# Threshold updates per tile, with new orders on ScalarE, GpSimd and TensorE, in a fused linear, top-k and layernorm kernel

## The chip, the cores and the metric

The kernel runs on one core of a Trainium2 chip. The metric is the device time of one execution in microseconds (us), the median of a few runs. The engines are TensorE (PE in the rows, PEld for its weight loads), VectorE (DVE), ScalarE (ACT), GpSimd (POOL) and the DMA queue that SyncE feeds (SP).

## The reference

What is computed, for 4096 tokens of 512 numbers:

```python
x = layernorm(x + x @ (W + delta_W).T)                      # x1
z = x @ ternary(W_syn).T + b_syn                            # 4096 x 2048
thresh = 204th largest of each row of z
hidden = where(z >= thresh, relu(z), 0)
out = hidden @ ternary(W_out).T + b_out
x = layernorm(layernorm(x + out, gamma, beta) + x)
```

`ternary` rounds a matrix to -1, 0 or +1 times its mean absolute value. The first term is one product, since the identity is added to `W + delta_W` in setup.

## The kernel before, in words

The tokens are cut into 32 tiles of 128. After a setup of about 50 us, each engine runs a list of steps written out by hand, a loop over stages `s` from 0 to 36, and works in each stage on several tiles at once: matmul 1 (`mm1`, fp32, 4 matmuls) on tile s+3, matmul 2 (`mm2`, 32 matmuls in two halves c=0 and c=1) on tile s+1, the copy of `z` out of PSUM (`evac`, two halves) on tile s, the selection (`below`, `top8`, `select`, `general`, `hidden`) on tile s-2, and matmul 3 (`mm3_hi` and `mm3_lo`, 16 matmuls each) on tile s-3. Each engine runs its own list strictly in order, and semaphores tie the lists together.

The 204th largest value of a row is searched for. ScalarE counts how many values of a row exceed a threshold (`count`, rounds 0 to 4, one pass over 2048 columns each), the threshold is moved after each count (after round 0 by `first_step` on ScalarE, after 1 to 3 by GpSimd), and VectorE then takes the eight largest values below the last threshold (`below`, `top8`) and picks the right one (`select`). `select` writes `ok`, and PE multiplies it by ones (`flags`), so that VectorE learns in `general` whether every row of the tile was found. Only then comes `hidden`, which zeroes what lies below the threshold. ScalarE rounds the result to fp16 (`hi_h`), VectorE makes the remainder (`lo_h`), and two DMA transposes bring both to `hT` for matmul 3 (their two arrivals are `hiT` and `loT`).

Before the change GpSimd moves the thresholds in a state of three columns, one for each tile in flight: `update_mid` moves one column after round 2, and `update_both` moves all three after the newest tile's round 1 and, with it, the older tile's round 3. A tile's `count` rounds are thereby spread over three stages: 0 and 1 in stage t, 2 and 3 in t+1, 4 in t+2.

Of the kernel before, what the change touches and what calls it, by code (L numbers as in the profile page):

```python
# [39 lines left out]
T_MIN = 1e-18  # L40
# [20 lines left out]
def postln_kernel(nc, x, xT, wT, dwT, w_synT, b_syn, w_outT, b_out, gamma, beta, out):  # L61
    ctx = ExitStack()
    with ctx:
# [155 lines left out]
        def mean_no(s):  # L219
            return s - L_LN2 + 1  # L220

        def count_no(t, r):

            s = t + (0, 0, 1, 1, 2)[r]
            whole = 2 * upto(s - 1) + 2 * upto(s - 2) + upto(s - 3)
            new, old, oldest = live(s), live(s - 1), live(s - 2)
            order = [2] * old + [4] * oldest + [3] * old + [0, 1] * new
            return whole + order.index(r) + 1
# [4 lines left out]
        def _(sp):  # L233
# [50 lines left out]
            for s in range(FIRST, LAST + 1):  # L284
                if live(s - L_MM3):
                    transpose_lo(s - L_MM3)
                if s % 2 and 2 <= (s + 5) // 2 < PAIRS:
                    load((s + 5) // 2)
                if live(s + A_LN1):
                    transpose_x(s + A_LN1)  # L290
                if live(s - L_OUT):
                    store(s - L_OUT)
                if live(s - L_SEL):
                    transpose_hi(s - L_SEL)
# [4 lines left out]
        def _(pool):  # L299
            g = nc.gpsimd  # L300
            made = 0
            for ap, value in ((ident, 0.0), (ones[:, :], 1.0), (cst[:, 0:3], -0.5), (cst[:, 3:4], 0.5),
                              (sums[:, :, :], 0.0), (ss[:, :, :], 0.0), (nmean[:, :, :], 0.0), (t_col[:, :, :], 0.0),
                              (ng[:, :], 0.0), (dev[:, :, :], 0.0), (signs[:, :], 0.0)):
                g.memset(ap, value).then_inc(pool_setup, 1)
                made += 1
# [27 lines left out]
            def means(s):  # L334
                j, d, e = s % 2, s - L_LN2, s - L_OUT
                wait(pool, r_made, upto(d))
                wait(pool, v_made, upto(e))
                wait(pool, sq_done[1], upto(d - 2))
                wait(pool, sq_done[2], upto(e - 2))
                g.tensor_scalar(nmean[:, j, :], sums[:, j, :], -1.0 / D, None, ALU.mult).then_inc(neg_means, 1)  # L340

            def scales(s):
                j, a, d, e = s % 2, s + A_LN1, s - L_LN2, s - L_OUT
                wait(pool, sq_done[0], upto(a))
                wait(pool, sq_done[1], upto(d))
                wait(pool, sq_done[2], upto(e))
# [3 lines left out]
                if live(e):  # L350
                    pool.wait_ge(rs_ready, ln_no(s))
                    g.tensor_tensor(b3[:, j:j + 1], nmean[:, j, 1:2], rs[:, j, 2:3], ALU.mult).then_inc(b3_ready, 1)
# [17 lines left out]
            def update(to, t_old, slope, signed, old, new):  # L370


                q = [tmp[:, k, 0:slope.shape[-1]] for k in range(8)]
                made_dev = step(g.tensor_scalar(new, signed, SIGN_MID, None, ALU.add))  # L374
                pool.wait_ge(update_step, made_dev)
                crossed = step(g.tensor_tensor(q[0], new, old, ALU.mult))
                squared = step(g.tensor_tensor(q[1], new, new, ALU.mult))
                pool.wait_ge(update_step, crossed)
                damp = step(g.tensor_scalar(q[2], q[0], 0.0, -DAMP, ALU.is_lt, ALU.mult))
                pool.wait_ge(update_step, squared)  # L380
                far = step(g.tensor_scalar(q[3], q[1], GATE ** 2, None, ALU.is_gt))
                pool.wait_ge(update_step, damp)
                less = step(g.tensor_tensor(q[4], q[2], slope, ALU.mult))
                pool.wait_ge(update_step, far)
                moved = step(g.tensor_tensor(q[5], q[3], new, ALU.mult))
                pool.wait_ge(update_step, less)
                damped = step(g.tensor_tensor(slope, slope, q[4], ALU.add))
                pool.wait_ge(update_step, max(damped, moved))
                by = step(g.tensor_tensor(q[6], q[5], slope, ALU.mult))  # L389
                pool.wait_ge(update_step, by)  # L390
                at = step(g.tensor_tensor(q[7], t_old, q[6], ALU.add))  # L391
                pool.wait_ge(update_step, at)
                return g.tensor_scalar(to, q[7], T_MIN, None, ALU.max)  # L393

            def update_mid(s, t):

                c = slice(t % CS, t % CS + 1)
                pool.wait_ge(counted, count_no(t, 2))
                update(t_col[:, s % 2, c], t_col[:, s % 2, c], ng[:, c], signs[:, c], dev[:, 1, c], dev[:, 0, c])\
                    .then_inc(updated_mid, 1)  # L400

            def reset(t):

                c = slice(t % CS, t % CS + 1)
                pool.wait_ge(counted, count_no(t, 0))
                step(g.tensor_copy(ng[:, c], start[:, 2:3]))  # L406
                g.tensor_scalar(dev[:, 0, c], sign_first[:, t % 2:t % 2 + 1], SIGN_MID, None, ALU.add).then_inc(t_reset, 1)
                pool.wait_ge(t_reset, t + 1)

            def update_both(s):  # L410

                if live(s):
                    pool.wait_ge(counted, count_no(s, 1))
                else:
                    pool.wait_ge(counted, count_no(s - 1, 3))
                wait(pool, updated_mid, upto(s - 1))
                wait(pool, selected, upto(s - 3))
                update(t_col[:, (s + 1) % 2, :], t_col[:, s % 2, :], ng[:, :], signs[:, :], dev[:, 0, :], dev[:, 1, :])\
                    .then_inc(updated, 1)

            for s in range(FIRST, LAST + 1):
                if s <= 2 and live(s + A_LN1):
                    scales(s)
                if s == -A_LN1:
                    bias_norm()
                if s == 0:
                    sigma()
                    scale_vecs()
# [5 lines left out]
                if live(s - L_SEL):  # L434
                    pool.wait_ge(masked, s - L_SEL + 1)
                if live(l):
                    if l == 0:
                        pool.wait_ge(vecs_made, 1)
                    add_bout(l)
                if live(d):  # L440
                    add_beta(d)
                if live(s):
                    reset(s)
                if live(s) or live(s - 1):
                    update_both(s)
                if live(d) or live(d - 1):
                    means(s + 1)

        @block.scalar
        def _(act):  # L450
# [51 lines left out]
            def count(s, t, r):  # L502
                if r == 0:
# [459 lines left out]
```

## Time and profile before

| | |
|---|---|
| median of 3 runs | 734.36 us (734.27 to 737.39) |
| the profiled execution | 738.88 us, span 736.8 us |
| busy: PE, DVE, ACT, POOL | 594.3, 542.7, 543.5, 470.4 us |
| mean granted TensorE clock | 0.943 of full |
| length of a stage in the steady part | 19.63 us |

The profiled execution lies 4.5 us above the median of the runs. Busy times overlap, so that they don't add up to the span; what bounds the kernel has to be read from the waits inside one stage. A row of the timeline gives the start, the duration, the engine, the line, the operation with what it writes and reads, and in brackets how long the engine had been idle and what ended that.

### The profile page before, as it was taken

How to read it: one execution, taken by the hardware profiler on the slowest of the kernel's cores; microseconds unless marked ns; L12 is line 12 of the kernel's file. 1: busy time of each engine (PE TensorE's matmuls, PEld its weight loads, DVE VectorE, ACT ScalarE, POOL GpSimd, SP SyncE). 2: the span in 40 equal slices, each digit the busy share in tenths (PEclk: the TensorE clock that was granted, in tenths of full speed). 3: DMA queues.
4: the chain of work that ended last, by engine and by line, in shares of the span. 5: the costliest groups of instructions: out<-in, count | busy, mean ns of one | idle time of the engine just before them, and what ended most of it. 6: DMA issues, size and time to landing. Idle time of an engine off the chain costs nothing.

```text
span 736.8 us, 8563 instructions
## 1 busy us (share of the span) xinstructions
PE 594.3 (81%) x2374; PEld 254.3 (35%) x2374; DVE 542.7 (74%) x650; ACT 543.5 (74%) x695; POOL 470.4 (64%) x1016
## 2 busy tenths in 40 slices
PE   0586579998888898899989899988888889874443
PEld 0132224443333333333333334433333333331111
DVE  4568486977777778788877777777777788886651
ACT  2753766778888888888888888888888888777422
POOL 0128556776767777776676677666676776676521
PEclk9988789999999999999999999999999999986676
DMA  8922034344455445555454443436454445433331
GB/s 347 384 53 59 0 64 95 65 99 72 108 86 115 79 97 82 115 87 115 86 111 90 81 101 73 98 79 116 85 94 86 80 86 86 86 72 72 71 74 40
DMA packets 184482, 71.63 MB, mean 97 GB/s; under 512 B 168048, under 2 KB 176240, under 8 KB 183792
## 3 DMA queue, kind: packets, MB, share of 16 engines
q1 hardware_dynamic: 184432, 71.07, 44.6%
q8 instruction: 19, 0.31, 0.2%
q14 instruction: 31, 0.25, 0.1%
HBM read 20.72 MB, written 8.39 MB: 40 GB/s over the span
## 4 chain that ended last, share of the span: by engine, by line
issue 33%; ACT 27%; POOL 24%; PE 7%; DMA 6%; DVE 2%; ACTq 1%; SPq 0%; POOLq 0%; DVEq 0%
ACT junk L525 12%; POOL tmp L389 8%; PE o_ps L886 3%; ACT y_sb L547 3%; POOL t_col L393 3%; DMA hT<-hh 2%; ACT junk_ln L499 2%; ACT x1s L537 2%; DMA z_sb<-in_w_synT 2%; ACT junk_ln L491 2%; POOL dev L374 2%; ACT junk_ln L483 2%; PE o_ps L892 2%; POOL tmp L391 2%; ACT t_col L531 2%
## 5 line engine op out<-in xcount | busy, mean ns | idle before, releaser
L525 ACT ACTIVATE junk<-z_sb,t_col 128x2048 f16<-128x2048 f32 x128 | 255.7, 1998 | 115.6 <-POOL t_col L393 114.5
L876 PE MATMUL z_ps<-t_syn,xhT 128*128 128x512 f16 x1024 | 231.1, 384 | 8.9 <-DMA xhT<-xh 6.4
L886 PE MATMUL o_ps<-t_out,hT 128*128 128x512 f16 x512 | 127.3, 406 | 76.3 <-DMA hT<-hh 76.3
L862 PE MATMUL u_ps<-weff,xT_sb 128*128 128x512 f32 x256 | 126.2, 638 | 34.3 <-ACT x1s L537 17.4
L876 PEld LDWEIGHTS z_ps<-t_syn,xhT 128*128 128x128 f16 x1024 | 101.2, 99 | 143.3 <-issue 33.3
L892 PE MATMUL o_ps<-t_out,hT 128*128 128x512 f16 x512 | 115.7, 379 | 0.5 <-DMA hT<-hh 0.5
L374 POOL TENSOR_SCALAR dev<-signs 128x3 f32<-128x3 f32 x65 | 63.5, 977 | 79.0 <-ACT junk L525 58.3
L886 PEld LDWEIGHTS o_ps<-t_out,hT 128*128 128x128 f16 x512 | 50.4, 103 | 151.8 <-DMA hT<-hh 84.6
L779 DVE SCALAR_TENSOR_TENSOR z_sb<-z_sb,thr 128x2048 f32<-128x2048 f32 x32 | 75.5, 2360 | 29.2 <-DVE flag L758 20.7
L406 POOL COPY ng<-start 128x1 f32<-128x1 f32 x32 | 50.9, 1591 | 65.4 <-ACT junk L525 65.4
L745 DVE SCALAR_TENSOR_TENSOR z_sb<-z_ps,sc,bias_z 128x1024 f32<-128x1024 f32 x64 | 79.5, 1277 | 14.8 <-PE z_ps L876 14.6
L752 DVE TENSOR_TENSOR xh<-x1s,xh 128x512 f16<-128x512 f32 x32 | 34.9, 1092 | 69.4 <-ACT xh L542 69.4
L713 DVE TENSOR_TENSOR hh<-z_sb,hh 128x2048 f16<-128x2048 f32 x32 | 73.3, 2292 | 12.4 <-ACT hh L554 12.0
L554 ACT ACTIVATE hh<-z_sb 128x2048 f16<-128x2048 f32 x32 | 60.7, 1897 | 26.8 <-DVE z_sb L779 26.7
L862 PEld LDWEIGHTS u_ps<-weff,xT_sb 128*128 128x128 f32 x256 | 49.2, 203 | 88.1 <-issue 87.9
L719 DVE SCALAR_TENSOR_TENSOR w_sb<-z_sb,t_col 128x2048 f32<-128x2048 f32 x32 | 75.0, 2345 | 0.3
L724 DVE MAX8 m<-w_sb 128x8 f32<-128x2048 f32 x32 | 73.4, 2295 | 1.1
L389 POOL TENSOR_TENSOR tmp<-tmp,ng 128x3 f32<-128x3 f32 x65 | 67.9, 1045 | 5.1
L892 PEld LDWEIGHTS o_ps<-t_out,hT 128*128 128x128 f16 x512 | 50.0, 98 | 61.2 <-DMA hT<-hh 1.0
L525 ACT ACTIVATE junk<-z_sb,start 128x2048 f16<-128x2048 f32 x32 | 63.7, 1989 | 1.0 <-DVE z_sb L745 1.0
L347 POOL TENSOR_SCALAR var<-ss 128x3 f32<-128x3 f32 x39 | 8.1, 207 | 53.8 <-ACT junk_ln L483 44.4
L357 POOL TENSOR_TENSOR x1b<-x1s,vecs 128x512 f32<-128x512 f32 x32 | 40.6, 1268 | 0.3 <-issue 0.2
(117 smaller groups left out, 640.1 us busy)
## 6 DMA issues: line engine op xcount, KB each, us to landing
xT_sb<-in_xT SPq DMA_DIRECT2D x16, 512.0 KB, 4.6
out_y<-y_sb SPq DMA_DIRECT2D x32, 256.0 KB, 2.4
z_sb<-in_w_synT SPq DMA_DIRECT2D x4, 1024.0 KB, 13.6
hh<-in_w_outT SPq DMA_DIRECT2D x2, 1024.0 KB, 18.9
z_sb<-in_w_outT SPq DMA_DIRECT2D x2, 1024.0 KB, 13.7
weff<-in_wT SPq DMA_DIRECT2D x1, 1024.0 KB, 5.7
w_sb<-in_dwT SPq DMA_DIRECT2D x1, 1024.0 KB, 7.9
bias_z<-in_b_syn SPq DMA_DIRECT2D x1, 1024.0 KB, 17.7
```

The costliest lines, as they stand in the source:

```text
L374: made_dev = step(g.tensor_scalar(new, signed, SIGN_MID, None, ALU.add))
L389: by = step(g.tensor_tensor(q[6], q[5], slope, ALU.mult))
L525: a_.activation(junk[:, n % 2, :], z_sb[:, t % ZS, :], ACT.Sign, bias=at, scale=-1.0, accum_out=signed)\
L713: v.tensor_tensor(hh[:, j, 1, :], z_sb[:, t % ZS, :], hh[:, j, 0, :], ALU.subtract).then_inc(h_lo, 1)
L719: v.scalar_tensor_tensor(w_sb[:, :], z, t_col[:, t % 2, t % CS:t % CS + 1], z, ALU.is_le, ALU.mult)\
L724: v.max(out=m8[:, t % 2, :], in_=w_sb[:, :]).then_inc(max8_done, 1)
L745: v.scalar_tensor_tensor(z_sb[:, t % ZS, c * HALF:(c + 1) * HALF], z_ps[:, c, :], sc[:, 7:8], bias_z[:, c * HALF:(c + 1) * HALF], ALU.mult ...
L779: v.scalar_tensor_tensor(z, z, thr[:, t % 2:t % 2 + 1], z, ALU.is_ge, ALU.mult).then_inc(h_made, 1)
L862: last = mm(u_ps[:, :], xT_sb[:, j, k, (t % 2) * P:(t % 2 + 1) * P], weff[:, k, :], start=k == 0, stop=k == KD - 1)
L876: last = mm(z_ps[:, c, b * BANK:(b + 1) * BANK], xhT[:, j, h * KD + k, :], t_syn[:, k, n0:n0 + BANK], start=k == 0 and h == 0, stop=k == K ...
L886: mm(o_ps[t % OS][:, :], hT[:, j, 0, c, :], t_out[:, c, :], start=c == 0, stop=False)
L892: last = mm(o_ps[t % OS][:, :], hT[:, j, 1, c, :], t_out[:, c, :], start=False, stop=c == KN - 1)
```

## The change

Each tile gets threshold state of its own (`t_col`, `slope`, `dev` and `signs` with a column for each round). `update(t, r)` replaces `update_mid` and `update_both`: seven instructions on one column for each of rounds 1, 2 and 3, where there were eleven, two times a stage. `reset` shrinks to `first_dev`. Round 4 now follows in stage t+1.

```diff
+            def update(t, r):
+                ...
+                pool.wait_ge(counted, count_no(t, r))
+                ...
+                crossed = step(g.tensor_scalar(q[0], signed, SIGN_MID, old, ALU.add, ALU.mult))
                 made_dev = step(g.tensor_scalar(new, signed, SIGN_MID, None, ALU.add))
+                pool.wait_ge(update_step, crossed)
+                damp = step(g.tensor_scalar(q[1], q[0], 0.0, -DAMP, ALU.is_lt, ALU.mult))
+                ...
+                g.tensor_scalar(t_col[:, j, r + 1:r + 2], q[3], slope[:, j, r:r + 1], t_col[:, j, r:r + 1],
+                                ALU.mult, ALU.add).then_inc(updated[r - 1], 1)
```

GpSimd's stage, before and after (`means` and `scales` now serve the second layernorm one stage earlier, tile s-3 in place of s-4, and the third tile s-4 in place of s-5; the wait for `masked` ahead of `add_bout` is gone; `scale_vecs` moves to VectorE in setup):

```diff
-                if live(s - 1):
-                    update_mid(s, s - 1)
-                if s > 2 and (live(s + A_LN1) or live(s - L_LN2) or live(s - L_OUT)):
-                    scales(s)
-                l, d = s + 1 - L_MM3, s + 1 - L_LN2
-                if live(s - L_SEL):
-                    pool.wait_ge(masked, s - L_SEL + 1)
...
-                    add_bout(l)
...
-                    add_beta(d)
...
-                    reset(s)
...
-                    update_both(s)
...
-                    means(s + 1)
+                if live(s - 1):
+                    update(s - 1, 3)
+                if live(l) or live(d):
+                    means(s)
+                if live(l):
+                    add_beta(l)
                 if live(s):
+                    first_dev(s)
+                    update(s, 1)
+                if live(l + 1):
...
+                    add_bout(l + 1)
+                if live(s + A_LN1) or live(l) or live(d):
                     scales(s)
                 if live(s):
+                    update(s, 2)
```

TensorE's stage:

```diff
                     mm3_hi(l)
-                    mm3_lo(l)
                 if live(f):
                     flags(s, f)
+                if live(l):
+                    mm3_lo(l)
                 if live(s + A_MM1):
                     mm1(s + A_MM1)
```

On VectorE the order of a stage stays (`lo_h`, both `evac`, `below`, `top8`, `select`, `lo_x`, `general`, `hidden`, then the layernorm steps); in the first stages one `sum_out` leaves it for ScalarE and `scale_vecs` comes. SyncE issues the transpose of `hi_h` ahead of the store and no longer behind it.

TensorE in the steady part, before the change. `u_ps` is matmul 1, `z_ps<-t_syn` matmul 2, `o_ps` matmul 3 (the two kinds of line are its high and its low half), `z_ps<-ok` the flags:

```order
66 L886 MATMUL o_ps<-t_out,hT 128x512 [waits y_ready,hiT1]
67 L886 MATMUL o_ps<-t_out,hT 128x512 x15
68 L892 MATMUL o_ps<-t_out,hT 128x512 [waits loT1]
69 L892 MATMUL o_ps<-t_out,hT 128x512 x15
70 L900 MATMUL z_ps<-ok,ones 1x1 [waits flag_read,z_evac,selected]
71 L862 MATMUL u_ps<-weff,xT_sb 128x512 [waits x1_ready,x_loaded0]
72 L862 MATMUL u_ps<-weff,xT_sb 128x512 x3
73 L876 MATMUL z_ps<-t_syn,xhT 128x512 [waits z_evac,flag_read,xT_done1]
```

The same engine with the change:

```order
44 L851 MATMUL o_ps<-t_out,hT 128x512 [waits hiT1]
45 L851 MATMUL o_ps<-t_out,hT 128x512 x15
46 L865 MATMUL z_ps<-ok,ones 1x1 [waits flag_read,z_evac,selected]
47 L857 MATMUL o_ps<-t_out,hT 128x512 [waits loT1]
48 L857 MATMUL o_ps<-t_out,hT 128x512 x15
49 L827 MATMUL u_ps<-weff,xT_sb 128x512 [waits x1_ready,x_loaded1]
50 L827 MATMUL u_ps<-weff,xT_sb 128x512 x3
51 L841 MATMUL z_ps<-t_syn,xhT 128x512 [waits z_evac,flag_read,xT_done1]
```

The flags matmul, with its wait for `selected`, now stands between the two halves of matmul 3; it stood behind both.

ScalarE in one steady stage before (`junk` rows are counts, `hh` is `hi_h`, `junk_ln` the squares, `x1s` and `xh` the first layernorm and its fp16 half, `y_sb` the output):

```order
101 L525 ACTIVATE junk,signs<-z_sb,t_col 128x2048
102 L525 ACTIVATE junk,sign_last<-z_sb,t_col 128x2048
103 L483 ACTIVATE junk_ln,ss<-u_ps 128x512
104 L491 ACTIVATE junk_ln,ss<-o_ps1,nmean 128x512
105 L499 ACTIVATE junk_ln,ss<-o_ps0,nmean 128x512
106 L525 ACTIVATE junk,signs<-z_sb,t_col 128x2048
107 L537 ACTIVATE x1s<-u_ps,rs 128x512
108 L542 ACTIVATE xh<-x1s 128x512
109 L547 ACTIVATE y_sb<-o_ps0,b3,rs 128x512
110 L525 ACTIVATE junk,sign_first<-z_sb,start 128x2048
111 L531 ACTIVATE t_col<-sign_first,start 128x1
112 L525 ACTIVATE junk,signs<-z_sb,t_col 128x2048
```

And with the change:

```order
100 L493 ACTIVATE junk,signs<-z_sb,start 128x2048
101 L493 ACTIVATE junk,signs<-z_sb,t_col 128x2048
102 L499 ACTIVATE t_col<-signs,start 128x1
103 L522 ACTIVATE hh<-z_sb 128x2048
104 L515 ACTIVATE y_sb<-o_ps0,b3,rs 128x512
105 L493 ACTIVATE junk,signs<-z_sb,t_col 128x2048 x2
106 L471 ACTIVATE junk_ln,ss<-o_ps1,nmean 128x512
107 L463 ACTIVATE junk_ln,ss<-o_ps2,nmean 128x512
108 L455 ACTIVATE junk_ln,ss<-u_ps 128x512
109 L493 ACTIVATE junk,signs<-z_sb,t_col 128x2048
110 L505 ACTIVATE x1s<-u_ps,rs 128x512
111 L510 ACTIVATE xh<-x1s 128x512
```

The newest tile's first count moved to the front, each tile's counts are separated by other work, and `hi_h` stands fourth where it stood last.

## Rows read from the trace of the kernel before

**Rows 1.** Busy time by stage: PE, PEld, DVE, ACT, POOL (instructions), PEclk, DMA share, GB/s
```profile
398.31:417.94 19.63, 17.77 (x76) 7.71 (x74) 15.54 (x18) 16.22 (x21) 13.84 (x31) 1.00 0.47 81
...
614.19:633.82 19.63, 15.95 (x68) 6.64 (x67) 15.53 (x18) 16.22 (x22) 13.84 (x31) 0.91 0.40 80
```

**Rows 2.** Who waited for whom: us in total, times, longest
```profile
ACT junk L525 <- POOL t_col L393: 114.5, 62, 7.7
```

**Rows 3.** Timeline of one steady stage, the wait on ScalarE
```profile
398.32 2.29 DVE L713 TENSOR_TENSOR hh<-z_sb,hh 128x2048 f16<-128x2048 f32 x1 [0.41 <-ACT hh L554]
398.43 2.24 POOL L389 TENSOR_TENSOR tmp<-tmp,ng 128x3 f32<-128x3 f32 x1
...
401.30 2.00 ACT L525 ACTIVATE junk<-z_sb,t_col 128x2048 f16<-128x2048 f32 x1 [3.02 <-POOL t_col L393]
```

**Rows 4.** Timeline, VectorE from the second evac to the selection
```profile
128.97 1.28 DVE L745 SCALAR_TENSOR_TENSOR z_sb<-z_ps,sc,bias_z 128x1024 f32<-128x1024 f32 x1 [1.66 <-PE z_ps L876]
130.18 2.34 DVE L719 SCALAR_TENSOR_TENSOR w_sb<-z_sb,t_col 128x2048 f32<-128x2048 f32 x1
132.55 2.29 DVE L724 MAX8 m<-w_sb 128x8 f32<-128x2048 f32 x1
134.88 0.22 DVE L731 TENSOR_SCALAR_CACHE_REDUCE pick<-place,sign_last 128x8 f32<-128x8 f32 x1
135.15 0.23 DVE L734 SCALAR_TENSOR_TENSOR ok<-m,t_col,hit 128x1 f32<-128x1 f32 x1
```

**Rows 5.** Timeline, TensorE in the same stretch
```profile
118.33 3.70 PE L862 MATMUL u_ps<-weff,xT_sb 128*128 128x512 f32 x8
121.87 7.07 PE L876 MATMUL z_ps<-t_syn,xhT 128*128 128x512 f16 x32
128.77 3.62 PE L886 MATMUL o_ps<-t_out,hT 128*128 128x512 f16 x16
132.23 3.62 PE L892 MATMUL o_ps<-t_out,hT 128*128 128x512 f16 x16
135.77 0.19 PE L900 MATMUL z_ps<-ok,ones 128*1 128x1 f32 x2
135.89 3.70 PE L862 MATMUL u_ps<-weff,xT_sb 128*128 128x512 f32 x8
```

**Rows 6.** Timeline, stage 2: selection, flags, and the wait before them
```profile
91.29 0.22 DVE L734 SCALAR_TENSOR_TENSOR ok<-m,t_col,hit 128x1 f32<-128x1 f32 x1
...
91.56 0.19 PE L900 MATMUL z_ps<-ok,ones 128*1 128x1 f32 x2 [8.61 <-DVE ok L734]
```

**Rows 7.** Timeline, TensorE at the end: idle gaps and what followed
```profile
610.21 7.07 PE L876 MATMUL z_ps<-t_syn,xhT 128*128 128x512 f16 x32
618.75 3.63 PE L886 MATMUL o_ps<-t_out,hT 128*128 128x512 f16 x16 [1.47 <-DMA hT<-hh]
...
628.16 8.75 PE L876 MATMUL z_ps<-t_syn,xhT 128*128 128x512 f16 x32 [2.21 <-issue]
...
645.86 7.07 PE L876 MATMUL z_ps<-t_syn,xhT 128*128 128x512 f16 x32 [0.29 <-issue]
656.79 6.40 PE L886 MATMUL o_ps<-t_out,hT 128*128 128x512 f16 x16 [3.87 <-DMA hT<-hh]
...
715.53 6.05 PE L886 MATMUL o_ps<-t_out,hT 128*128 128x512 f16 x16 [9.88 <-DMA hT<-hh]
```

**Rows 8.** Timeline, TensorE in the first stages
```profile
60.97 0.38 PE L904 MATMUL o_ps<-part_out,ones 128*128 128x1 f32 x2 [1.59 <-DVE part_out L694]
...
69.44 6.61 PE L862 MATMUL u_ps<-weff,xT_sb 128*128 128x512 f32 x8 [4.62 <-ACT x1s L537]
```

**Rows 9.** DMA issues: median us from issue to landing
```profile
hT<-hh SPq DMA_TRANSPOSE x3, 4.4
```

**Rows 10.** Timeline, the last full stages: general, hidden and hi_h
```profile
628.92 2.35 DVE L779 SCALAR_TENSOR_TENSOR z_sb<-z_sb,thr 128x2048 f32<-128x2048 f32 x1 [0.86 <-DVE flag L758]
...
631.95 1.90 ACT L554 ACTIVATE hh<-z_sb 128x2048 f16<-128x2048 f32 x1
```

More of the change, by code:

```diff
@@ L219, in mean_no @@
         def mean_no(s):
-            return s - L_LN2 + 1
+            return s - L_MM3 + 1
         def count_no(t, r):
[L224 to L227, printed above, removed]
+            s = t + (r > 2)
+            whole = 3 * upto(s - 1) + 2 * upto(s - 2)
+            new, old = [0] * live(s), [3] * live(s - 1)
+            order = new + old + [1] * live(s) + [4] * live(s - 1) + [2] * live(s)
             return whole + order.index(r) + 1
@@ L368, in step, with first_dev @@
                 return steps_made[0]
-            def update(to, t_old, slope, signed, old, new):
-                q = [tmp[:, k, 0:slope.shape[-1]] for k in range(8)]
+            def first_dev(t):
+                pool.wait_ge(counted, count_no(t, 0))
+                g.tensor_scalar(dev[:, t % 2, 0:1], signs[:, t % 2, 0:1], SIGN_MID, None, ALU.add).then_inc(dev_made, 1)
+            def update(t, r):
+                j = t % 2
+                signed, new, old = signs[:, j, r:r + 1], dev[:, j, r:r + 1], dev[:, j, r - 1:r]
+                before = slope[:, j, r - 1:r] if r > 1 else start[:, 2:3]
+                q = [tmp[:, k:k + 1] for k in range(4)]
+                pool.wait_ge(counted, count_no(t, r))
+                if r == 1:
+                    pool.wait_ge(dev_made, t + 1)
+                crossed = step(g.tensor_scalar(q[0], signed, SIGN_MID, old, ALU.add, ALU.mult))
@@ L380, in update @@
+                pool.wait_ge(update_step, damp)
+                damped = step(g.tensor_scalar(slope[:, j, r:r + 1], q[1], before, before, ALU.mult, ALU.add))
                 pool.wait_ge(update_step, squared)
[L381 to L408, printed above, removed]
@@ new lines, in update @@
+                far = step(g.tensor_scalar(q[3], q[2], GATE ** 2, new, ALU.is_gt, ALU.mult))
+                pool.wait_ge(update_step, max(damped, far))
+                if r == ROUNDS - 2:
+                    wait(pool, selected, t - 1)
+                g.tensor_scalar(t_col[:, j, r + 1:r + 2], q[3], slope[:, j, r:r + 1], t_col[:, j, r:r + 1],
+                                ALU.mult, ALU.add).then_inc(updated[r - 1], 1)
+                pool.wait_ge(updated[r - 1], t + 1)
+            scales(-3)
@@ L601, in _ @@
                 if live(s):
-                    count(s, s, 0)
-                    first_step(s, s)
-                    count(s, s, 1)
-                if live(f):
-                    hi_h(f)
+                    count(s, 1)
+                if live(s - 1):
+                    count(s - 1, 4)
+                if live(d):
+                    square3(s, d)
+                if live(l):
+                    square2(s, l)
+                if live(a):
+                    square1(s, a)
+                if live(s):
+                    count(s, 2)
+                if live(a):
+                    ln1_out(s, a)
+                    hi_x(a)
         @block.vector
@@ L819, in _ @@
                     evac(s, 0)
+                    evac(s, 1)
                 if s == 1:
@@ L822, in _ @@
                     out_weights(0)
-                if live(s):
-                    evac(s, 1)
-                if s == 0:
-                    lo_x(a)
-                    sum_out(2)
-                    sum_out(3)
-                    out_part()
-                if s == 1:
-                    lo_x(a)
-                    out_weights(1)
                 if live(f):
@@ L836, in _ @@
                     select(f)
-                if live(a) and s > 1:
+                if live(a):
                     lo_x(a)
-                if s == 2:
-                    out_weights(2)
+                if s == 0:
+                    sum_out(3)
+                    scale_vecs()
+                    out_part()
+                if s == 1:
+                    out_weights(1)
                 if live(f):
```

228 lines of the change are left out of this document (98 added, 130 removed).

## The prediction, made before the changed kernel ran

> **What bounds the kernel now.** I read the busy times by stage first. In a steady stage PE is busy 17.77 us of 19.63, ScalarE 16.22, VectorE 15.54, GpSimd 13.84 [rows 1]: no engine is full, so a loop of waits sets the pace. The list of waits puts 114.5 us on ScalarE, in 62 waits for a threshold from GpSimd [rows 2]. The timeline shows one: ScalarE idles 3.02 us until `update_both` is through [rows 3]. One small GpSimd instruction of that chain takes 2.24 us, while VectorE's `lo_h` of 2.29 us runs beside it [rows 3]. So today's loop runs through ScalarE's counts and GpSimd's two updates, and PE, 1.47 us idle per stage before matmul 3, is close behind [rows 7]. The GPSIMD Engine Reference of the Trainium skill, section 1 (Specifications), says that GpSimd shares its SBUF interfaces with VectorE, with contention where VectorE has two SBUF inputs; the stretched row agrees.
>
> The steady pace to compare with: matmul 2 of one tile ends at 121.87 + 7.07 = 128.94 and that of the tile 25 stages later at 610.21 + 7.07 = 617.28 [rows 5, 7], so 19.53 us a stage.
>
> **The change, part by part.** *GpSimd and ScalarE.* The two updates of eleven instructions become three of seven, on one column, and ScalarE has other work between the counts of one tile. I cost the ScalarE stall as gone: the engine's own work of 16.22 us [rows 1] is then its floor, and GpSimd's 13.84 falls by what is no longer stretched. This cover holds as long as a stage lasts longer than about 16.5 us. The early place of `hi_h` makes ScalarE wait for `hidden` of the same stage. Behind it are queued `ln3_out`, two counts, the squares, the last count, `x1s` and `xh`; VectorE's next `lo_h` and matmul 3 wait for it. From `lo_h` to the end of `hidden` VectorE has lo_h 2.29, two evacs 2.47 (1.21 pitch and 1.28), below and max8 4.70, select about 0.7, lo_x 0.7 to 1.1, the flag 1.0 and hidden 2.35, some 14.4 us; with `hi_h`, 1.90 [rows 3, 4, 10], that loop needs about 16.4 us. It doesn't bind while another loop needs more.
>
> *TensorE.* This part decides. `flags` waits for `select` of tile s-2, which VectorE makes after the second `evac` of the stage, `below` and `top8`. And that evac waits for the end of matmul 2, the last thing PE did in its stage before. Before the change PE had both halves of matmul 3 to do in the meantime: they begin at 128.77 and PE reaches the flags at 135.77, while `select` is ready at 135.15 + 0.23 = 135.38 [rows 4, 5]. The wait cost nothing, by 0.4 us. Now only the high half stands ahead of it, and PE must stand idle; `mm3_lo`, `mm1` and `mm2` are queued behind, and VectorE's next second evac waits for those. This closes a loop of exactly one stage:
> - second evac to `ok`: from 128.97 to 135.15, and 0.23: 6.41 us [rows 4]
> - `ok` to the flags: 91.56 - 91.29 - 0.22 = 0.05 [rows 6]
> - flags to the next matmul: 0.12 [rows 5]
> - `mm3_lo`: 3.46, the pitch of 16 such matmuls from 128.77 to 132.23 [rows 5]
> - `mm1`: 3.54, from 118.33 to 121.87 [rows 5]
> - `mm2`: 7.07, and 0.03 until the evac [rows 4, 5]
>
> Together 20.68 us, against 19.53 now: +1.15 in each of 25 steady stages, +28.8 us. Without the move of the flags this loop would be 20.68 - 3.46 = 17.2 us. Nothing on GpSimd and ScalarE can shorten it, and both have over 4 us of room in it.
>
> *The clock of TensorE.* In this loop PE stands idle in every stage from 128.77 + 3.62 = 132.39 (end of the high half) until the flags at 128.97 + 6.41 + 0.05 = 135.43: 3.04 us. The trace shows the granted clock 1.00 with gaps of 1.47 us, 25 times [rows 1, 7]. After a gap of 2.21 us the next 32 matmuls took 8.75 us instead of 7.07 (+1.68), in the stage with a granted clock of 0.91 [rows 1, 7]; after 3.87 us the next 16 took 6.40 instead of 3.63 (+2.77) [rows 7]. These are stretches of the 1.2 GHz level in place of 2.4. The new gap lies between the two that were followed by a fall. The bounds are 0 and 2.77 per stage; I take 1.68. The new gap is as far from the one row as from the other (0.83 us each), and I choose the cheaper, because it leaves room for stages in which the clock doesn't fall: 25 x 1.68 = +42.0 us. TensorE: Matmul & The Clock Gate of the Trainium skill, section "HAM oscillation", warns of a kernel that went back to the slower clock in each pass of its loop, since it waited in each; this is the rule that speaks against the change, and the rows above agree with it.
>
> *Stages 29 and 30* have no `mm1` left: 20.68 - 3.54 + 1.68 = 18.82 each, together 37.6. Before it is from 617.28 to 645.86 + 7.07 = 652.93, or 35.65 [rows 7]: +2.0 us.
>
> *The first stages.* PE waited 4.62 us for `x1s`, which stood behind a count that waited for GpSimd, and 1.59 us for `part_out`, behind a `sum_out` that now goes to ScalarE [rows 8]. Before the first flags it waited 8.61 [rows 6]; the path from matmul 2 to `ok` needs 6.49 as above, so 2.1 comes off. Together -8.3 us. The bounds are 0 (new waits in their place) and -14.8, all three waits gone whole; I take the sum since GpSimd now has fewer and shorter steps there.
>
> *The end.* After the last matmul 2 (652.93) nothing fills PE. The four high halves of matmul 3 follow until 715.53 [rows 7], 62.6 us. Each tile's counts now end a stage earlier, so that ScalarE and GpSimd no longer hold the chain. After the last matmul 2: 6.5 to the flags, about 1.2 to `hidden`, 2.35, `hi_h` 1.90, the transpose 4.4, so 16.4 to the high half of tile 29. For tiles 30 and 31 each: high half 6.2 (of 6.40 and 6.05), flags and general 1.3, hidden 2.35, hi_h 1.95, transpose 4.4, so 16.2 [rows 4, 7, 9, 10]. In sum 48.8: -13.8 us. Behind tile 31's matmul 3 I leave the chain as it is (736.8 - 715.53 = 21.3). Bounds: 0 and -18.
>
> SyncE's transpose ahead of the store, and `means` and `scales` one stage earlier, I cost at nothing: the transpose arrives 4.4 us after its issue [rows 9], and PE wants it over 8 us later in a stage of 20.7. `add_bout`, which no longer waits for `masked`, falls into VectorE's idle time before the second evac; if it met `below` it could hold it 1.3 us, on the loop.
>
> **Sum.** +28.8 +42.0 +2.0 -8.3 -13.8 = +50.7 us. The profiled execution, 738.88 us, would become 789.6; against the median of the runs, 734.36, it gives **785 us**.
>
> **The rivals.**
> - *The clock stays up.* Same loop, no fall: 785 - 42 - 3 = 740, up to about 750 with a fall now and then. For it: the gap moves in time from stage to stage, and 1.47 us never did harm. Against it: both gaps over 2 us. Some 20%, and 10% for something between, 750 to 773.
> - *The clock falls longer*, 2.77 a stage: 785 + 27 x 1.1 = 815. 4%.
> - *PE doesn't wait at the flags (the other sign).* If `select` were ready when the high half ends, that is within 3.5 us of the end of matmul 2, in place of 6.5, the ScalarE stall would be all that changed, and PE's own 17.77 with some 0.4 us of seams would set the pace: 18.2 a stage, 734 - 25 x 1.35 - 22 = 678. For it: the stall of 3.02 us really goes. Against it: evac 1.21, below 2.37 and max8 2.33 stand in VectorE's list ahead of `select` [rows 4], unchanged. It decides if that order, or the wait of the second evac for matmul 2, were not as I read them. 5%.
> - *GpSimd's chain still binds*, since VectorE's long instructions stretch its small ones: that would need over 4 us more a stage than now. 2%; it would add to the 785.
>
> **How the numbers follow.** The forecast with the fall in nearly every stage has 60%, with 774 to 797 as its own range (first stages and end off by a few us each, the clock's price 1.3 to 2.0). About 0.5% is what a measurement of this kernel tells from no change, 730.7 to 738.0 us. Faster: 6% (the PE rival and an end better than I think). Same: 5% (clock up, first stages or end better by 5 us). Slower: 89%. The range reaches down to the case of the steady clock, 741, and up to 799; about 2 in 10 lie outside.
>
> **What would show it.** In the changed kernel's profile: PE idle about 3 us ahead of the flags in each stage, ended by VectorE's `ok`; ScalarE's long wait for `t_col` gone, replaced by a wait for `hidden` at `hi_h`; VectorE idle some 2 us ahead of the second evac, ended by matmul 2; a granted clock below 1.00 in the steady stages, and `mm3_lo` or `mm1` sometimes long. A stage of 22.4 us shows the whole, 20.7 the loop alone. Wrong would be a pace under 20 us, or the wait ahead of the flags ended by something else than `ok`.

## The result, and the profile after

The changed kernel takes **778.67 us** (median of four runs, 765.82 to 781.07), against 734.32 for the kernel before on the same chip: a ratio of 1.049 (95% interval 1.036 to 1.062). The ratio is made from the two quicker runs, 776.42 and 765.82 us, whose median is 771.12, so that the 65 and 23 us worked out below from the median of all four would be 58 and 16 against these. TensorE's mean granted clock was 0.909, 0.909, 0.913 and 0.929 in the four runs, in the order of falling time. The forecast was 785 us, with a range of 741 to 799, and a chance of 89% for slower. The profiled run took 780.93 us, with a span of 779.1.

The page of the changed kernel: busy time, the granted clock in 40 slices, and the chain that ended last.
```profile
PE 614.4 (79%) x2374; PEld 262.6 (34%) x2374; DVE 527.0 (68%) x649; ACT 546.6 (70%) x697; POOL 539.9 (69%) x936
...
PEclk9789789999999999999999999999999999997666
...
PE 55%; DVE 22%; POOL 8%; issue 8%; DMA 3%; ACT 2%; DVEq 0%; POOLq 0%; SPq 0%; ACTq 0%
PE z_ps L841 24%; PE o_ps L857 16%; PE u_ps L827 13%; DVE w_sb L687 8%; DVE m L692 8%; PE o_ps L851 2%; POOL t_col L392 1%; POOL dev L380 1%; DMA hT<-hh 1%; DMA xhT<-xh 1%; DMA w_sb<-in_dwT 1%; POOL tmp L379 1%; DVE pick L700 1%; ACT junk L493 1%; DVE ok L703 1%
```
The chain names the loop by itself, all but the second `evac`, whose time it counts as issue: `mm2` (L841), `below` (L687), `max8` (L692), `ok` (L703), `mm3_lo` (L857), `mm1` (L827). The high half of matmul 3 (L851) stands in it with 2% only, since it lies beside VectorE's part.

Who waited for whom, the changed kernel: us in total, times, longest.
```profile
DVE z_sb L714 <- PE z_ps L841: 153.5, 57, 5.5
ACT hh L522 <- DVE z_sb L748: 103.7, 29, 7.8
PE z_ps L865 <- DVE ok L703: 91.0, 30, 6.5
...
ACT junk L493 <- POOL t_col L392: 60.1, 39, 5.3
```
ScalarE's 114.5 us for a threshold [rows 2] have become 60.1, in shorter pieces; its long wait is now for `hidden` at `hi_h` (L522). PE waits 91.0 us, 30 times, for `ok` at the flags.

The timeline of TensorE in the changed kernel, three stages.
```profile
352.17 7.07 PE L841 MATMUL z_ps<-t_syn,xhT 128*128 128x512 f16 x32
359.07 3.62 PE L851 MATMUL o_ps<-t_out,hT 128*128 128x512 f16 x16
365.72 0.19 PE L865 MATMUL z_ps<-ok,ones 128*1 128x1 f32 x2 [3.03 <-DVE ok L703]
365.84 5.31 PE L857 MATMUL o_ps<-t_out,hT 128*128 128x512 f16 x16
370.99 3.60 PE L827 MATMUL u_ps<-weff,xT_sb 128*128 128x512 f32 x8
374.43 7.07 PE L841 MATMUL z_ps<-t_syn,xhT 128*128 128x512 f16 x32
...
387.98 0.19 PE L865 MATMUL z_ps<-ok,ones 128*1 128x1 f32 x2 [3.03 <-DVE ok L703]
388.10 5.07 PE L857 MATMUL o_ps<-t_out,hT 128*128 128x512 f16 x16
...
396.44 7.07 PE L841 MATMUL z_ps<-t_syn,xhT 128*128 128x512 f16 x32
...
410.00 0.19 PE L865 MATMUL z_ps<-ok,ones 128*1 128x1 f32 x2 [3.03 <-DVE ok L703]
410.12 3.63 PE L857 MATMUL o_ps<-t_out,hT 128*128 128x512 f16 x16
```
In each stage PE stands idle 3.03 us ahead of the flags. Then `mm3_lo` takes 3.63 us, or 5.31, or 5.07: after two of three gaps the clock is down for a while. From matmul 2 to matmul 2 the stages last 22.26, 22.01 and, without a fall, 20.57 us, in this order again and again.

By stretch, the changed kernel: 25 steady stages, stages 29 and 30, and the end (columns as in [rows 1]).
```profile
120.49:662.93 542.44, 466.63 (x1851) 201.51 (x1850) 377.40 (x450) 407.63 (x527) 410.93 (x702) 0.94 0.42 83
662.93:698.90 35.97, 29.90 (x132) 12.69 (x130) 29.66 (x35) 25.09 (x29) 27.44 (x44) 0.95 0.30 58
698.90:779.00 80.10, 37.19 (x134) 14.20 (x134) 41.98 (x55) 35.63 (x50) 47.53 (x76) 0.71 0.33 70
```
The sum on the spans of the two profiled runs (736.8 to 779.1 us, +42.3), each part beside what was forecast:

| part | before | after | difference | forecast |
|---|---|---|---|---|
| start, to the end of tile 4's matmul 2 | 128.94 | 120.49 | -8.45 | -8.3 |
| 25 steady stages | 488.34 | 542.44 | +54.1 | +70.8 |
| of it the loop, 25 x (20.57 - 19.53) | | | +26.0 | +28.8 |
| of it the clock, the rest | | | +28.1 | +42.0 |
| stages 29 and 30 | 35.65 | 35.97 | +0.3 | +2.0 |
| the end | 83.9 | 80.2 | -3.7 | -13.8 |

### The profile page after: what moved, and what is told of

It is laid out like the page before. It is cut to its first block, busy times and chain, and to the rows that moved or that the text cites. A ratio compares the mean times of both kernels' runs of the same rounds, so it can differ in the third digit from the quotient of the medians.

```text
span 779.1 us, 8524 instructions
## 1 busy us (share of the span) xinstructions
PE 614.4 (79%) x2374; PEld 262.6 (34%) x2374; DVE 527.0 (68%) x649; ACT 546.6 (70%) x697; POOL 539.9 (69%) x936
## 4 chain that ended last, share of the span: by engine, by line
PE 55%; DVE 22%; POOL 8%; issue 8%; DMA 3%; ACT 2%; DVEq 0%; POOLq 0%; SPq 0%; ACTq 0%
PE z_ps L841 24%; PE o_ps L857 16%; PE u_ps L827 13%; DVE w_sb L687 8%; DVE m L692 8%; PE o_ps L851 2%; POOL t_col L392 1%; POOL dev L380 1%; DMA hT<-hh 1%; DMA xhT<-xh 1%; DMA w_sb<-in_dwT 1%; POOL tmp L379 1%; DVE pick L700 1%; ACT junk L493 1%; DVE ok L703 1%
## 5 line engine op out<-in xcount | busy, mean ns | idle before, releaser
L493 ACT ACTIVATE junk<-z_sb,t_col 128x2048 f16<-128x2048 f32 x128 | 255.4, 1996 | 61.2 <-POOL t_col L392 60.1
L841 PE MATMUL z_ps<-t_syn,xhT 128*128 128x512 f16 x1024 | 228.7, 382 | 5.0 <-DMA xhT<-xh 5.0
L714 DVE SCALAR_TENSOR_TENSOR z_sb<-z_ps,sc,bias_z 128x1024 f32<-128x1024 f32 x64 | 82.0, 1283 | 153.5 <-PE z_ps L841 153.5
L851 PE MATMUL o_ps<-t_out,hT 128*128 128x512 f16 x512 | 126.0, 403 | 34.6 <-DMA hT<-hh 34.6
L841 PEld LDWEIGHTS z_ps<-t_syn,xhT 128*128 128x128 f16 x1024 | 100.5, 98 | 138.3 <-issue 26.2
L857 PE MATMUL o_ps<-t_out,hT 128*128 128x512 f16 x512 | 145.8, 449 | 0.0
L827 PE MATMUL u_ps<-weff,xT_sb 128*128 128x512 f32 x256 | 124.1, 630 | 22.6 <-DVE weff L608 16.8
L522 ACT ACTIVATE hh<-z_sb 128x2048 f16<-128x2048 f32 x32 | 61.1, 1909 | 103.7 <-DVE z_sb L748 103.7
L379 POOL TENSOR_SCALAR tmp<-signs,dev 128x1 f32<-128x1 f32 x96 | 68.9, 718 | 89.2 <-ACT junk L493 80.7
L335 POOL TENSOR_SCALAR nmean<-sums 128x2 f32<-128x2 f32 x33 | 62.2, 1886 | 49.3 <-DVE o_ps L769 47.5
L851 PEld LDWEIGHTS o_ps<-t_out,hT 128*128 128x128 f16 x512 | 52.1, 103 | 104.1 <-DMA hT<-hh 31.6
L857 PEld LDWEIGHTS o_ps<-t_out,hT 128*128 128x128 f16 x512 | 55.0, 112 | 76.5 <-issue 39.2
L865 PE MATMUL z_ps<-ok,ones 128*1 128x1 f32 x64 | 6.0, 164 | 91.0 <-DVE ok L703 91.0
L827 PEld LDWEIGHTS u_ps<-weff,xT_sb 128*128 128x128 f32 x256 | 51.4, 203 | 78.1 <-issue 74.4
L687 DVE SCALAR_TENSOR_TENSOR w_sb<-z_sb,t_col 128x2048 f32<-128x2048 f32 x32 | 76.0, 2376 | 0.5 <-POOL t_col L392 0.5
L692 DVE MAX8 m<-w_sb 128x8 f32<-128x2048 f32 x32 | 73.4, 2295 | 1.1
L388 POOL TENSOR_SCALAR tmp<-tmp,dev 128x1 f32<-128x1 f32 x96 | 63.9, 666 | 9.4
L386 POOL TENSOR_SCALAR slope<-tmp,slope 128x1 f32<-128x1 f32 x64 | 62.4, 974 | 0.0
L392 POOL TENSOR_SCALAR t_col<-tmp,slope,t_col 128x1 f32<-128x1 f32 x96 | 44.4, 462 | 9.5
```

The source lines that it names most:

```text
L379: crossed = step(g.tensor_scalar(q[0], signed, SIGN_MID, old, ALU.add, ALU.mult))
L388: far = step(g.tensor_scalar(q[3], q[2], GATE ** 2, new, ALU.is_gt, ALU.mult))
L493: a_.activation(junk[:, n % 2, :], z_sb[:, t % ZS, :], ACT.Sign, bias=at, scale=-1.0, accum_out=signs[:, j, r:r + 1]).then_inc(counted, 1)
L687: v.scalar_tensor_tensor(w_sb[:, :], z, t_col[:, t % 2, ROUNDS - 1:ROUNDS], z, ALU.is_le, ALU.mult)\
L692: v.max(out=m8[:, t % 2, :], in_=w_sb[:, :]).then_inc(max8_done, 1)
L714: v.scalar_tensor_tensor(z_sb[:, t % ZS, c * HALF:(c + 1) * HALF], z_ps[:, c, :], sc[:, 7:8], bias_z[:, c * HALF:(c + 1) * HALF], ALU.mult ...
```

## The experiments

All change one thing in the changed kernel, if not said otherwise. The kernel before ran beside each of them, with medians of 733.94 (the first four), 735.64 (`e5` to `e8`), 737.19 (`e9`) and 735.24 us (`e10`, `e11`).

**e1_flags_behind: the one suspected part undone.**
```diff
                     mm3_hi(l)
+                    mm3_lo(l)
                 if live(f):
                     flags(s, f)
-                if live(l):
-                    mm3_lo(l)
```


> The changed kernel with the flags matmul put back behind both halves of matmul 3, everything else of the change kept. My theory (the early flags close a loop of 20.6 us): PE's idle time ahead of the flags (91 us in the changed kernel) goes, the loop falls to about 17.1 us, PE's own work sets the pace, about 18.2 us a stage at a granted clock of 1.00, and the time is some 680 to 695 us, below the kernel before. Rival (the new ScalarE and GpSimd orders are what slows the kernel): it stays above 750 us.

Measured: 713.52 us (712.22 to 714.59), ratio 0.972 (0.968 to 0.976). With the flags back in their old place the change makes the kernel *quicker* than before, by 2.8%. The place of the flags is worth 778.67 - 713.52 = 65 us, and all the rest of the change, without it, about -20. Yet it isn't the 680 to 695 that I had expected. The timeline of three engines in one stage:
```profile
395.73 0.26 POOL L379 TENSOR_SCALAR tmp<-signs,dev 128x1 f32<-128x1 f32 x1 [2.37 <-ACT junk L493]
...
397.70 2.46 POOL L392 TENSOR_SCALAR t_col<-tmp,slope,t_col 128x1 f32<-128x1 f32 x1
...
403.05 2.33 POOL L384 TENSOR_SCALAR tmp<-dev 128x1 f32<-128x1 f32 x1
...
406.58 2.00 ACT L493 ACTIVATE junk<-z_sb,t_col 128x2048 f16<-128x2048 f32 x1 [2.37 <-POOL t_col L392]
...
408.27 0.88 POOL L344 TENSOR_TENSOR rs<-var,cst 128x3 f32<-128x3 f32 x1
409.18 0.69 ACT L505 ACTIVATE x1s<-u_ps,rs 128x512 f32<-128x512 f32 x1 [0.51 <-POOL rs L344]
410.01 3.67 PE L827 MATMUL u_ps<-weff,xT_sb 128*128 128x512 f32 x8 [0.85 <-ACT x1s L505]
...
414.32 0.19 ACT L493 ACTIVATION_READ_ACCUMULATOR junk<-z_sb,t_col 128x1 f32 x1
```
PE no longer waits for `ok`, but for `x1s`. A new loop of one stage binds. GpSimd does update 3, `means`, `add_beta`, `first_dev`, update 1, `add_bout` and `scales` with hardly a pause, from 395.73 until `rs` is there at 409.15, 13.4 us; two of its small instructions are stretched to 2.46 and 2.33 us where they elsewhere take 0.34 and 0.29. ScalarE has waited 0.51 us for `rs` and then does `x1s`, `xh` and the next stage's first two counts, from 409.18 to 414.51, 5.3 us; the second of these counts starts GpSimd's next update 3. With the seams that is the stage, 18.95 us in most of them, and no longer PE's 18.2. ScalarE's longer wait, 2.37 us for the threshold, lies inside this loop and does not set its pace: behind it ScalarE still waited for `rs`.

**e2_before_flags_mid: this part done alone, in the kernel before** (the diff of `e1` turned round).

> The kernel before with only the flags matmul moved between the two halves of matmul 3. My theory: the same loop of 20.6 us arises there, PE waits 3 us ahead of the flags in each stage and its clock falls in most; pace 21.5 to 22, time 780 to 800 us. Rival: the old update chain of 19.6 us with its slack hides the move, 734 to 745 us.

Measured: 775.96 us (773.10 to 778.15), ratio 1.056 (1.051 to 1.061), a little under the 780 to 800 that I had expected. Its timeline of TensorE:
```profile
413.97 0.19 PE L900 MATMUL z_ps<-ok,ones 128*1 128x1 f32 x2 [3.03 <-DVE ok L734]
414.10 5.32 PE L892 MATMUL o_ps<-t_out,hT 128*128 128x512 f16 x16
```
The same gap, and the same stages of 20.58, 22.26 and 22.01 us. Once this loop binds, nothing that the rest of the change does to ScalarE and GpSimd is seen in the steady stages.

**e3_fill12 and e8_fill6: the clock apart from the loop.** Ahead of the high half PE does 12 (or 6) of its matmuls once more; the next start overwrites them, so that the output is the same.
```diff
                 wait(pe, y_ready, t - OS + 1)
+                for c in range(12):
+                    mm(o_ps[t % OS][:, :], hT[:, j, 0, c, :], t_out[:, c, :], start=c == 0, stop=c == 12 - 1)
                 for c in range(KN):
```


> The changed kernel with 12 matmuls more ahead of the high half of matmul 3 (a repetition of its first 12, overwritten by the real ones), so that PE works 2.6 of the 3.03 us in which it waited for the flags. The loop isn't touched, only the idle time. If the clock's fall is a cost of its own: granted clock 1.00 in the steady stages, stages of 20.6 us, time 745 to 755 us. Rival (the long low halves come from something else, say the flags matmul or memory traffic): 775 or more.

> The changed kernel with 6 matmuls more ahead of the high half of matmul 3, which leaves 1.75 us of idle time ahead of the flags, between the 1.47 us that left the clock up and the 2.21 us after which it fell once. If a gap must be near 2.2 us: granted clock 1.00 in the steady stages and 750 to 757 us. If the fall begins below that: some low halves of 5 us, 757 to 775.

Measured: 755.55 us with 12 (754.64 to 757.35), ratio 1.028 (1.025 to 1.032), at the upper end of what I had expected, and 754.07 with 6 (one run), as expected. The timeline of TensorE with 12:
```profile
411.09 2.75 PE L851 MATMUL o_ps<-t_out,hT 128*128 128x512 f16 x12
413.68 3.62 PE L853 MATMUL o_ps<-t_out,hT 128*128 128x512 f16 x16
417.74 0.19 PE L867 MATMUL z_ps<-ok,ones 128*1 128x1 f32 x2 [0.44 <-DVE ok L703]
417.86 3.63 PE L859 MATMUL o_ps<-t_out,hT 128*128 128x512 f16 x16
```
and with 6:
```profile
414.88 0.19 PE L867 MATMUL z_ps<-ok,ones 128*1 128x1 f32 x2 [1.74 <-DVE ok L703]
415.00 3.63 PE L859 MATMUL o_ps<-t_out,hT 128*128 128x512 f16 x16
```
More work in the gap and less time: each stage is now 20.57 us, at a granted clock of 1.00. That is the loop without the clock, and the clock's share is 778.67 - 755.55 = 23 us. A gap of 1.74 us leads to no fall either.

**e4_flags_first: a larger dose**, the flags ahead of both halves.
```diff
+                if live(f):
+                    flags(s, f)
                 if live(l):
...
                     mm3_hi(l)
-                if live(f):
-                    flags(s, f)
-                if live(l):
                     mm3_lo(l)
```


> The changed kernel with the flags matmul ahead of both halves of matmul 3: a larger dose. My theory: the loop grows by 3.46 us to 24.0 and PE's idle time ahead of the flags to 6.5 us, a fall of the clock in every stage adds 1.5 to 3; pace 25.5 to 27, time 870 to 910 us. If the loop were not the cause, the time would stay near 780 us.

Measured: 905.71 us (one run), within the 870 to 910 expected, granted clock 0.843. The timeline of TensorE:
```profile
395.97 0.19 PE L865 MATMUL z_ps<-ok,ones 128*1 128x1 f32 x2 [6.48 <-DVE ok L703]
396.09 4.97 PE L851 MATMUL o_ps<-t_out,hT 128*128 128x512 f16 x16
```
The whole path from matmul 2 to `ok` is now a gap, 6.48 us, as the forecast's 6.41 of VectorE and its seams say. Stages last 25.4, 26.3 and 26.8 us, and now the clock falls in each.

**e5_tail: the end.** The end had gained 3.7 us in place of 13.8. The changed kernel's timeline after its last matmul 2 shows where `hi_h` stood:
```profile
707.30 2.36 DVE L748 SCALAR_TENSOR_TENSOR z_sb<-z_sb,thr 128x2048 f32<-128x2048 f32 x1 [1.22 <-issue]
707.61 2.14 POOL L380 TENSOR_SCALAR dev<-signs 128x1 f32<-128x1 f32 x1
...
711.54 2.00 ACT L493 ACTIVATE junk<-z_sb,t_col 128x2048 f16<-128x2048 f32 x1 [3.13 <-POOL t_col L392]
713.82 1.89 ACT L522 ACTIVATE hh<-z_sb 128x2048 f16<-128x2048 f32 x1
720.04 6.34 PE L851 MATMUL o_ps<-t_out,hT 128*128 128x512 f16 x16 [10.58 <-DMA hT<-hh]
```
`hidden` was ready at 709.66, but `hi_h` began 4.2 us later, queued behind round 3 of tile 30's counts, which waited for a GpSimd update that `hidden` itself had stretched (2.14 us for a small instruction). The experiment puts `hi_h` ahead of that count, from stage 31 on.
```diff
                     count(s, 0)
+                if live(f) and s >= TILES - 1:
+                    hi_h(f)
                 if live(s - 1):
                     count(s - 1, 3)
...
-                if live(f):
+                if live(f) and s < TILES - 1:
                     hi_h(f)
```


> The changed kernel with hi_h moved ahead of count round 3 on ScalarE in the last stages alone (from stage 31). My theory of the missing gain at the end: hidden of tiles 29 and 30 was done at 709.7 and 729.9 us, but hi_h began 4.1 and 4.2 us later, behind a count that waited for GpSimd. Then the stretch from the last matmul 2 to the end shrinks from 80.2 to about 72 us. Rival (the transposes or the slow clock of matmul 3 set the end): within 1.5 us of 80.

Measured: 777.12 us (one run), and 75.2 us from the end of the last matmul 2, against 80.2: neither the 72 of my theory nor the rival's 80. The high half of tile 29 comes 16.8 us after matmul 2 (forecast 16.4). But tile 30's waits for `y_sb`, since `ln3_out` is now what stands behind the count that waits for GpSimd:
```profile
733.07 2.00 ACT L493 ACTIVATE junk<-z_sb,t_col 128x2048 f16<-128x2048 f32 x1 [3.79 <-POOL t_col L392]
...
735.97 5.00 PE L853 MATMUL o_ps<-t_out,hT 128*128 128x512 f16 x16 [9.37 <-ACT y_sb L515]
```
So 5 of the missing 10 us are shown to be this queue. Of the rest, tile 30 took 2.8 us more than forecast, with this wait for `y_sb` ahead of it, and tile 31 1.8 us more, which was not followed up.

**e6, e7, e9, e10, e11: GpSimd's order, all on top of e1.** These ask whether the loop of 18.95 us can be cut. `e10` and `e11` ran on another chip than the rest. GpSimd's order in a stage of `e1` is update 3, means, add_beta, update 1, add_bout, scales, update 2.
- `e6_beta_late`: add_beta behind update 1. `e7_beta_tail`: the same, with the edit of `e5`
- `e9_scales_early`: update 1, scales, add_bout, add_beta, update 2
- `e10_bout_between`: update 1, scales, add_bout, update 2, add_beta
- `e11_adds_last`: update 1, scales, update 2, add_bout, add_beta

The edit of `e6`; the others are of the same kind.
```diff
-                if live(l):
-                    add_beta(l)
                 if live(s):
                     first_dev(s)
                     update(s, 1)
+                if live(l):
+                    add_beta(l)
```


> The changed kernel with the flags behind both halves of matmul 3, and on GpSimd add_beta behind update(s, 1) in place of ahead of it. With the flags back a stage took 18.95 us, and ScalarE waited 2.37 us for update(s, 1), which stood behind add_beta (1.27 us) and was then stretched by below (2.33). My theory: that wait sets the pace there; it goes, PE's own 17.8 and seams take over, 18.2 to 18.5 a stage, time 698 to 706 us. Rival (DMA arrival of hT or the hidden, hi_h, lo_h loop sets it): 711 to 715.

> The kernel of the run before with hi_h ahead of count round 3 in the last stages too. If both theories hold: 6 to 9 us below it, 690 to 699. If the end is set by something else: the same time.

> The changed kernel with the flags behind both halves of matmul 3, and on GpSimd both adds (add_bout, then add_beta) behind update(s, 1) and scales(s). With add_beta late alone the wait moved: ScalarE's wait for update(s, 1) fell from 2.37 to 1.20 us, but its wait for rs from scales rose from 0.51 to 1.78, and the pace stayed at 18.9. My theory: GpSimd's order, with its instructions stretched by VectorE, still sets the pace; with scales early too the x1s step comes 1.5 us or more sooner and the pace falls to 18.0 to 18.4, 694 to 703 us. Rival (DMA arrival of hT, or the hidden, hi_h, lo_h loop): 709 to 714 again.

> Flags behind both halves, GpSimd's stage in the order update 3, means, update 1, scales, add_bout, update 2, add_beta. In the run before, update 2 began behind both adds at 413.4 us and fell under hidden (one step of 0.34 took 2.46), so that count round 3, hi_h and lo_h came 3 us late and the pace was 20.7. My theory: with one add behind update 2 it is through before hidden begins, while scales stays early: pace 18.0 to 18.5, 695 to 704 us. If an early scales itself were what hurt: 745 to 755 again. If something off GpSimd holds the pace at 18.9: 710 to 714.

> The same with both adds behind update 2. My theory: update 2 is early, but now update 3 of the next stage stands behind the adds; as it is not urgent (its count has 6 us until select), 695 to 706 us, near the run with add_bout between. If update 3 is what matters: 712 or more.

| kernel | us | range | ratio to before |
|---|---|---|---|
| e6_beta_late | 712.72 | 711.96 to 714.63 | 0.970 (0.965 to 0.974) |
| e7_beta_tail | 712.22 | 711.90 to 717.04 | 0.970 (0.965 to 0.976) |
| e9_scales_early | 753.46 | 752.01 to 754.08 | 1.024 (1.021 to 1.026) |
| e10_bout_between | 722.13 | 720.82 to 724.55 | 0.983 (0.979 to 0.986) |
| e11_adds_last | 719.58 | 719.44 to 719.72 | 0.978 (0.976 to 0.981) |

None of the five met the forecast of my theory; `e6`, `e7` and `e11` came out at the time given for another cause. Two waits on ScalarE's timeline of `e6` show why the first did nothing:
```profile
405.41 2.00 ACT L493 ACTIVATE junk<-z_sb,t_col 128x2048 f16<-128x2048 f32 x1 [1.20 <-POOL t_col L392]
...
409.29 0.69 ACT L505 ACTIVATE x1s<-u_ps,rs 128x512 f32<-128x512 f32 x1 [1.78 <-POOL rs L344]
```
The wait for the threshold fell from 2.37 to 1.20 us, and that for `rs`, whose `scales` stood behind the moved addition, rose from 0.51 to 1.78. The sum stays (2.88 and 2.98), and so does the pace, 19.0 us: the loop goes through `rs` and `x1s`, as it did in `e1`, and ahead of `rs` nothing had been taken away. My number for the rival (711 to 715) was met, by this cause and not the one I had named. At the end `e7` took 84.5 us for the 84.1 of `e6`: no gain.

The timeline of `e9` shows what an order can cost:
```profile
411.30 0.74 DVE L703 SCALAR_TENSOR_TENSOR ok<-m,t_col,hit 128x1 f32<-128x1 f32 x1
411.97 1.31 DVE L705 SCALAR_TENSOR_TENSOR pick<-place,signs,m 128x8 f32<-128x8 f32 x1
...
414.81 2.35 DVE L748 SCALAR_TENSOR_TENSOR z_sb<-z_sb,thr 128x2048 f32<-128x2048 f32 x1 [0.86 <-DVE flag L727]
414.92 2.46 POOL L386 TENSOR_SCALAR slope<-tmp,slope 128x1 f32<-128x1 f32 x1
...
418.26 2.00 ACT L493 ACTIVATE junk<-z_sb,t_col 128x2048 f16<-128x2048 f32 x1 [3.62 <-POOL t_col L392]
...
422.46 2.29 DVE L681 TENSOR_TENSOR hh<-z_sb,hh 128x2048 f16<-128x2048 f32 x1 [3.10 <-ACT hh L522]
...
426.78 3.63 PE L851 MATMUL o_ps<-t_out,hT 128*128 128x512 f16 x16 [3.00 <-DMA hT<-hh]
```
Update 2, now behind both additions, falls beside `hidden`, one of its small instructions takes 2.46 us, and the delay runs through the count, `hi_h` and `lo_h` to PE: 20.74 us in this stage, 18.1 to 23.7 in the steady ones. VectorE is held up as well: beside GpSimd's two additions (`add_bout` from 410.76, `add_beta` from 411.99) `ok` took 0.74 us and the `pick` behind it 1.31, in place of 0.22 each in `e1`. `e10` differs from `e9` only in that update 2 stands ahead of `add_beta`, and gets 31 us back. So the order of these two is shown to be the cause; whether by the late update 2 or by the longer `pick`, which is back at 0.22 us in `e10`, is not told apart. `e10` and `e11` stay above `e1`. In `e10` it is `add_beta` that meets `hidden`:
```profile
417.12 2.39 DVE L748 SCALAR_TENSOR_TENSOR z_sb<-z_sb,thr 128x2048 f32<-128x2048 f32 x1 [1.24 <-issue]
417.46 3.19 POOL L356 TENSOR_TENSOR x1g<-x1s,vecs 128x512 f32<-128x512 f32 x1
```
The quickest kernels of all are `e1`, `e6` and `e7`, whose ranges overlap.

## Why the prediction was right, point by point

- **The loop through the flags.** Right, and shown by undoing it (`e1`, -65 us), doing it alone (`e2`, +42) and the larger dose (`e4`, +127). The gap was 3.03 us (forecast 3.04) and the stage without a fall 20.57 (20.68). The rival in which PE doesn't wait is out.
- **The clock, 1.68 in each stage.** Right in kind and too large in size, the term most off: +28.1 us in the profiled run and 23 by `e3` (its extra matmuls also lengthen the end, 83.6 us for 80.2), not 42.0. A fall costs what I took, 1.69 or 1.44, but comes after two gaps of three. I had put "nearly every stage" on record as the likeliest, with the row of 2.21 us, a single case, as its only price. The section on HAM oscillation in TensorE: Matmul & The Clock Gate of the Trainium skill speaks of a fall in each pass; here it was two in three at 3.03 us, and each at 6.48.
- **The rival "the clock stays up"** (740 to 750) did not come. The run of 765.82 us, at a granted clock of 0.929, falls in the range of the case between (750 to 773, 10%). No profile of it was kept, so how often the clock fell in it is not known.
- **ScalarE's stall "gone".** Partly. 60.1 us of waits for `t_col` are left. They cost nothing in steady stages as long as a stage lasts 20.6 us, for those of `e2` are as long; in `e1` GpSimd's loop binds. Here the forecast's floor was wrong: it held the cover to last down to 16.5 us a stage, from ScalarE's busy time and the loop through `hi_h`. The loop of GpSimd's updates, additions and `rs` with ScalarE's `x1s` and counts needs 18.95, and I had not added it up: the room in a stage of 20.57 was 1.6 us, and not over 4. The case of 678 us shared this fault: without the wait at the flags the kernel takes 713.5.
- **The first stages.** -8.45 for -8.3, in part by luck. The wait ahead of the first flags was 6.49 us, as worked out; that for `part_out` is gone, and that for `x1s` fell from 4.62 to 0.66 us. But `mm1` behind it took 3.67 us in place of 6.61 [rows 8], 2.9 us that I had not counted. A new wait of 1.57 us for `x1s`, a longer `mm1` behind it (6.58 for 5.75) and small losses at the first matmul 3 took about as much away.
```profile
62.60 3.67 PE L827 MATMUL u_ps<-weff,xT_sb 128*128 128x512 f32 x8 [0.66 <-ACT x1s L505]
...
81.42 6.58 PE L827 MATMUL u_ps<-weff,xT_sb 128*128 128x512 f32 x8 [1.57 <-ACT x1s L505]
```
- **The end.** -3.7 for -13.8: the step "ScalarE and GpSimd no longer hold the chain" failed. `hi_h` stood behind a count that waited for GpSimd, which accounts for 5 of the missing 10 us (`e5`). The rival "GpSimd's chain still binds" was thus true of the end of the changed kernel, and not of its steady stages, with its reason: VectorE's long instructions stretch small ones.
- **At nothing** I had costed the transpose ahead of the store, `means` and `scales` earlier, and `add_bout`; nothing in `e2`'s steady stages, equal to those of the changed kernel, speaks against it.

The +14 us that the clock's term had too much and the +5 of the loop and stages 29 and 30 were set off by the 10 us that the end did not give: part of the closeness of 785 to 778.67 is luck.

Open: why `e10` and `e11` stay above `e1` was not settled stage by stage. Their traces show VectorE held up beside GpSimd's additions (`ok` 0.74 us, the median of 32, in `e10`; `hidden` 3.1 to 3.3 us in place of 2.35 in some stages of `e11`), but no run takes that away alone; and the ratios of `e11` and `e1` touch at 0.976. Whether GpSimd's loop falls below PE's 18.2 us once its two stretched instructions run beside something else was not tried.

## What to carry to other kernels

On an engine that works in order, the place of an instruction that waits decides how long the loop through it is: move one ahead of 3.5 us of independent work, and that work is added to the loop; where this loop becomes the longest, as here, stalls that go elsewhere don't help. Count each loop of one stage by itself (here three: through the flags, through `hi_h`, and through GpSimd's updates and additions, `rs` and ScalarE's counts), for once the longest is cut the next binds, and cover must be asked of that one, not of busy times. Where small instructions share a stage with long ones of another engine, look up beside what each falls before moving it; the same work took 713 or 753 us.

## What the runs showed of the hardware

- **GpSimd's small instructions.** On one column they take 0.2 to 0.35 us, but 2.1 to 2.5 when one begins just before or under `lo_h`, `below` or `hidden` of VectorE (2.3 us, two operands in SBUF): they end 0.1 to 0.2 us after VectorE's instruction. Beside `max8` (one operand) and `evac` (from PSUM) they don't; so one stretched instruction per meeting, whatever their number. GpSimd's addition of 1.27 us took 3.19 in `e10`. It works the other way too: beside the two additions of `e9` VectorE's `ok` and `pick` took 0.74 and 1.31 us in place of 0.22, and beside those of `e11` `hidden` took up to 3.26 in place of 2.35. I had expected the first effect from [rows 3], not that two stretched instructions would lie in the loop that paces `e1`.
- **The clock has a regular beat at a regular gap.** At gaps of 3.03 us, in the changed kernel and `e2` alike, the pattern is fall (1.69), fall (1.44), none. Gaps of 0.44, 0.85 and 1.74 us brought none in steady stages, 6.48 one in each stage. The length of a gap alone does not tell whether a fall follows: in `e9` the high half of matmul 3 took 3.63 us behind gaps of 3.43 and 3.00 us, and 5.31 behind one of 2.98. In `e1`, the changed kernel and `e4` PE's work in a stage is the same and only the idle time differs (0.32 and 0.85, 3.03, 6.48 us); in `e3` and `e8` there is also more work, so that gap and work aren't told apart there.
